# Weights of the weighing read from PSUM, and the last eight tiles weighed ahead of the scores, in a five-pass graph network kernel

## The chip, the cores and the metric

The kernel runs on one core of a Trainium2 chip. The metric is the device time of one execution in microseconds. Before the change the median of three runs is 8032.57 us.

## What is computed

The reference is a stack of four graph layers over 6250 nodes with 256 features each and 106250 edges, sorted by the node they end in. Each layer gathers a 256-wide row for every edge's source, weighs it, sums the rows per destination, and adds a normalised result to the node's features. The layers differ in how the weight of an edge is found. The first and the last use given or degree-based weights. The second is an attention with 8 heads, the third has a 4-head graph attention followed by a 1-head one. Of these two kinds the core is:

```
sim = (q[:, dst] * k[:, src]).sum(-1) * scale        # 8 heads
e   = leaky_relu(es[src] + ed[dst], 0.2)             # 4 heads, then 1 head
m   = segment_max(e, dst);  w = exp(e - m[dst])
out = segment_sum(w * h[src], dst) / segment_sum(w, dst)
```

The change touches the product `w * h[src]` of the 8-head and of the 4-head part.

## The kernel before

The edges are cut into tiles of 128. There are five passes over all tiles, L = 0 to 4: plain sum, 8-head, 4-head, 1-head, plain sum, each followed by a stage over the nodes. The 8-head pass takes the tiles in 55 batches of 16; the 4-head pass takes 27 batches of 32 and a last one of 16.

**The ring.** GpSimd issues one indirect DMA for each tile (line 770), which gathers the 128 source rows into a slot of a ring in SBUF (`ring`, here `rg`). In a slot lie the 256 values and, behind them, columns for the weights of the heads (from `po_` on). Before each group of four gathers GpSimd waits until TensorE has summed the tiles that stood in these slots (`p["agg"]`).

**A batch in the 4-head pass.** The passes are pipelined in software: one step computes the scores of batch b and the sums of batch c = b - 1. The weights go through a chain over four engines:

- VectorE adds up the scores, `scores_of` (lines 1701, 1704, 1706), and signals `s`.
- TensorE turns them into `m0[0:R, 0:128]`, the PSUM bank 6, `turn_scores` (1223, 1224), and signals `st`.
- VectorE scans along the tiles, `ch1` (1785, 1788); TensorE picks rows (1242 to 1244) and signals `row`; VectorE's `ch2` works on them (1805 to 1817); TensorE turns them again (1250, 1251); VectorE's `ch3` (1823 to 1831) leaves the differences from the maxima.
- ScalarE takes the exponential (932, 933, 935), TensorE turns the result back into `m0[:, 128:128 + R]` (`turn_back`, 1256), the other part of the same bank, and ScalarE copies it from there to the ring's weight columns (943) and signals `w`.

In the 8-head pass bank 3 has the part of `m0`, TensorE also spreads the queries over the edges (1188), and VectorE's `pair` multiplies them with the keys (1687) and adds the products up (1678).

**The sums.** VectorE's `begin_sums` (1858, 1859) waits for `w` and for all earlier sums. Then `weigh` (1838) multiplies a tile's values in the ring by its weights, in place, before TensorE multiplies the tile with a one-hot matrix of its destinations (1107). VectorE adds each result to an accumulator in SBUF (1619 in the 4-head pass, 1616 in the 8-head pass). TensorE's sum of tile k waits for the weighing of its group of four (`wv`), for the one-hot, which ScalarE makes (878, 881), and for VectorE's add a few tiles back.

Which engine weighs which tile is written out by hand. In the 4-head pass VectorE weighs all: `prepare_four(g)` is one instruction of 128x1024 for four tiles, `add_and_prepare(g, n)` puts two instructions of 128x512 for group n between the four adds of group g. In the 8-head pass VectorE weighs the first four tiles (`weigh_four(0)`), GpSimd the next four (783) and ScalarE the last eight (909). The 1-head pass has no weighing: there VectorE writes weighted one-hots (`hot_some`).

The order on VectorE in a full step of the 4-head and of the 1-head pass is: `begin_sums`, `prepare_four(0)`, `prepare_four(1)`, sixteen adds with groups 2 to 5 between them, `scores_of`, `prepare_four(6)`, `load_offsets`, `ch1`, adds 16 to 19, `prepare_four(7)`, `ch2`, adds 20 to 23, `ch3`, adds 24 to 31.

TensorE's order is: the sums of tiles 0 to 15, `turn_scores`, sums 16 to 19, the rows for `ch2` (1242 to 1244), sums 20 to 23, the columns for `ch3` (1250, 1251), sums 24 to 27, `turn_back`, sums 28 to 31.

Of the kernel before, what the change touches and what calls it, by code (L numbers as in the profile page):

```python
# [160 lines left out]
def gnn_kernel(nc, a, out):  # L161
    ctx = ExitStack()
    with ctx:
# [1237 lines left out]
        def _(dve):  # L1401
# [158 lines left out]
            for L in range(5):  # L1560
# [87 lines left out]
                else:  # L1648
# [184 lines left out]
                    def weigh(c, rset, k, n):  # L1833

                        four = rg[:, rset * G + k:rset * G + k + n, :]
                        vv = four[:, :, po_ - 256:po_].rearrange("p s (h d) -> p s h d", h=H)
                        wv = four[:, :, po_:po_ + H].unsqueeze(3).to_broadcast([128, n, H, 256 // H])
                        return tt(vv, vv, wv, ALU.mult)  # L1838

                    def hot_some(c, cp, k, n):  # L1840
# [24 lines left out]
                    def batch(i, o, scores, sums):  # L1865
# [38 lines left out]
                        if L == 1:  # L1904
                            pair(0)
                            dots(0)
                            if sums:
                                begin_sums(c, window_at(cp, 0), cp)
                            weigh_four(0)
                            if scores:  # L1910
                                load_offsets(b, par, 0)
                            pair(1)
                            add(0, 1)
                            dots(1)
                            add(1, 3)
                            pair(2)
                            add(3, 4)
                            dots(2)
                            add(4, 5)
                            pair(3)  # L1920
                            add(5, 6)
                            dots(3)
                            add(6, 7)
                            if scores:
                                scan_forward(b, par, ub)
                            add(7, 8)
                            if scores:
                                scan_backward(b, par)
                            add(8, 9)
                            if feed:  # L1930
                                compare_turned(b + 1, (o + 1) % 2)
                            if scores:
                                rows_forward(b, par)
                            add(9, 10)
                            if scores:
                                rows_backward(b, par)
                            add(10, 11)
                            if scores:
                                rows_most(b)
                            add(11, 12)  # L1940
                            if scores:
                                rows_before(b)
                            add(12, 13)
                            if scores:
                                limit_before(b, par)
                            add(13, 14)
                            if scores:
                                limit_behind(b, par)
                            add(14, 15)
                            if scores:  # L1950
                                carry(b)
                            add(15, 16)
                            if scores:
                                differences(b)
                        elif sums and short(L, c):
                            begin_sums(c, window_at(0, 0), cp)
                            prepare_four(0)
                            prepare_four(1)
                            add_and_prepare(0, 2)
                            add_and_prepare(1, 3)  # L1960
                            add(8, 16)
                        else:
                            if sums:
                                begin_sums(c, window_at(0, 0), cp)
                            prepare_four(0)
                            if sums:
                                load_offsets(c, 1, 16)
                            prepare_four(1)
                            add_and_prepare(0, 2)
                            add_and_prepare(1, 3)  # L1970
                            add_and_prepare(2, 4)
                            add_and_prepare(3, 5)
                            if scores:
                                scores_of(b, rset, use, par)
                            prepare_four(6)
                            if scores:
                                load_offsets(b, 0, 0)
                                ch1(b, par, ub)
                            add(16, 20)
                            prepare_four(7)  # L1980
                            if scores:
                                ch2(b, par)
                            add(20, 24)
                            if scores:
                                ch3(b, par)
                            add(24, 32)
# [171 lines left out]
```

## Time and profile before

| | |
|---|---|
| median of the runs | 8032.57 us (8017.61 to 8053.89, three runs) |
| the profiled execution | 8040.43 us |
| its span | 8038.4 us, mean granted TensorE clock 0.76 |
| busy over the span | TensorE 57%, VectorE 54%, GpSimd 58%, ScalarE 31% |
| 8-head pass | about 1637 to 3345 us |
| 4-head pass | about 3552 to 4950 us |
| 1-head pass | about 5130 to 6560 us |

The span is the time from the first to the last record of the profile. What lies around it in the profiled execution is 8040.43 - 8038.4 = 2.0 us. The profiled execution is 7.9 us above the median and lies within the spread of the runs. No engine is busy for more than six tenths of the span, so the time is made of waits of the engines on each other, and the busy shares alone don't say what an instruction on one of them is worth.

### The profile page before, as it was taken

What the parts mean: (1) busy time and instruction counts of PE and PEld (TensorE: products, weight loads), DVE (VectorE), ACT (ScalarE), POOL (GpSimd) and SP (SyncE); (2) the same over time, 40 slices, a digit from 0 to 9 for tenths busy, and PEclk for the clock granted to TensorE, in tenths of its full rate; (3) what the DMA queues carried; (4) which work ended last, traced back from release to release, by engine and by line L of the source; (5) the groups of instructions that cost most, each with busy time, mean ns of one, the idle gap of its engine ahead of it and who ended that gap; (6) DMA issues with size and microseconds to landing.
All of it is one profiled execution on the core that took longest, in us unless ns stands there. A gap on an engine that the chain in (4) does not pass through costs nothing.

```text
span 8038.4 us, 108779 instructions
## 1 busy us (share of the span) xinstructions
PE 4559.5 (57%) x23715; PEld 3453.3 (43%) x23716; DVE 4305.4 (54%) x11140; ACT 2505.5 (31%) x7576; POOL 4682.6 (58%) x5273
## 2 busy tenths in 40 slices
PE   3444446778877787845555556344444463444445
PEld 2444444455555555633333334233333343444444
DVE  4444445567766777735555557344444462444446
ACT  0000000267766777534444445211111130000003
POOL 4666664655555555566666664555555546666661
PEclk6777777889888999967777768667667676777776
DMA  3333332566666666543333333333333343333332
GB/s 87 89 89 89 88 88 70 182 183 197 197 189 183 190 200 189 131 135 112 105 108 109 105 108 63 114 103 100 94 100 102 100 107 107 89 89 88 89 89 85
DMA packets 498682, 953.01 MB, mean 119 GB/s; under 512 B 104802, under 2 KB 298501, under 8 KB 491191
## 3 DMA queue, kind: packets, MB, share of 16 engines
q0 software_dynamic: 235232, 683.41, 31.0%
q1 hardware_dynamic: 263157, 266.87, 10.6%
q14 instruction: 253, 2.07, 0.1%
q8 instruction: 40, 0.66, 0.0%
HBM read 885.36 MB, written 65.90 MB: 118 GB/s over the span
## 4 chain that ended last, share of the span: by engine, by line
PE 37%; DVE 22%; another core or an unknown queue 20%; issue 13%; DVEq 5%; ACT 1%; SPq 1%; DMA 1%; POOL 0%; ACTq 0%; POOLq 0%
PE bank L1107 16%; DVE acc L1635 7%; PE bank L1104 5%; PE bank L1133 4%; DVE ohc L1625 4%; DVE acc L1619 3%; PE bank L1390 2%; PE bank L1186 1%; PE bank L1187 1%; PE bank L1188 1%; DVEq L1604 1%; DVEq L1633 1%; DVE ring L1838 1%; DVE acc L1616 1%
## 5 line engine op out<-in xcount | busy, mean ns | idle before, releaser
L770 POOL DMA_INDIRECT ring<-g_t,stage x1760 | 1736.2, 986 | 1133.0 <-issue 475.8
L1107 PE MATMUL bank<-ring,ohc 128*128 128x264 f32 (+2 forms) x5280 | 1825.2, 477 | 841.7 <-DVE ohc L1843 295.1
L1104 PE MATMUL bank<-ohc,ring 128*128 128x128 f32 x6656 | 1171.6, 352 | 1324.4 <-DVE acc L1635 1233.5
L1104 PEld LDWEIGHTS bank<-ohc,ring 128*128 128x128 f32 x6656 | 1100.4, 260 | 1396.1 <-DVE acc L1635 1305.3
L1107 PEld LDWEIGHTS bank<-ring,ohc 128*128 128x128 f32 x5280 | 1113.4, 235 | 1136.0 <-issue 742.1
L1619 DVE TENSOR_TENSOR acc<-acc,bank 128x261 f32 (+1 forms) x1760 | 747.2, 425 | 1113.5 <-remote 561.4
L770 POOL DMA_INDIRECT ring<-kv_t,stage x880 | 874.8, 994 | 705.3 <-PE bank L1107 409.6
L1625 DVE TENSOR_SCALAR ohc<-iota,rel_c,relx 128x128 f32<-128x128 f32 x1664 | 474.1, 353 | 1183.7 <-remote 878.4
L770 POOL DMA_INDIRECT ring<-in_x,stage x832 | 793.8, 954 | 434.9 <-issue 213.3
L770 POOL DMA_INDIRECT ring<-xs_t,stage x832 | 795.3, 956 | 419.1 <-issue 216.3
L1635 DVE TENSOR_TENSOR acc<-acc,bank 128x256 f32 x1664 | 698.8, 420 | 194.1 <-DVE acc L1635 135.0
L909 ACT ACTIVATE ring<-ring 128x32 f32<-128x32 f32 x3520 | 751.2, 306 | 0.8 <-issue 0.8
L878 ACT ACTIVATE ohc<-iota,rel_c 128x128 f32<-128x128 f32 x1760 | 560.5, 389 | 346.9 <-remote 172.9
L932 ACT ACTIVATE cl<-cl 128x1 f32<-128x1 f32 (+3 forms) x111 | 22.5, 203 | 1960.1 <-issue 916.8
L1133 PE MATMUL bank<-ident 128*128 128x256 bf16 x3410 | 540.7, 292 | 118.4 <-DVE acc L1616 109.1
L1616 DVE SCALAR_TENSOR_TENSOR acc<-acc,aux,bank 128x264 f32 x880 | 423.1, 481 | 314.5 <-PE bank L1107 185.4
L1133 PEld LDWEIGHTS bank<-ident 128*128 128x128 bf16 x3410 | 331.2, 104 | 295.2 <-DVE acc L1616 158.8
L957 ACT ACTIVATE acc<-aux,cols 128x512 f32<-128x512 f32 (+1 forms) x26 | 16.7, 690 | 1294.7 <-DVE aux L2027 1294.7
L961 ACT ACTIVATE acc<-bank 128x512 f32<-128x512 f32 (+1 forms) x13 | 7.4, 573 | 1253.4 <-PE bank L1326 1253.4
L1223 PE MATMUL bank<-ident,sc 128*128 128x128 f32 (+3 forms) x112 | 37.9, 441 | 581.7 <-DVE sc L1706 497.5
L1838 DVE TENSOR_TENSOR ring<-ring 128x512 f32<-128x512 f32 (+1 forms) x385 | 352.8, 917 | 7.2
L1687 DVE TENSOR_TENSOR aux<-bank,ring 128x1024 f32<-128x1024 f32 x220 | 268.5, 1220 | 143.9 <-remote 65.8
(331 smaller groups left out, 6329.5 us busy)
## 6 DMA issues: line engine op xcount, KB each, us to landing
aux<-relb_t SPq DMA_DIRECT2D x56, 1024.0 KB
aux<-q_t SPq DMA_DIRECT2D x880, 64.0 KB
relx<-relb_t SPq DMA_DIRECT2D x55, 512.0 KB
ring<-g_t,stage POOLq DMA_INDIRECT x1760
x<-ring SPq DMA_DIRECT2D x21, 896.0 KB, 4.2
ring<-x SPq DMA_DIRECT2D x21, 896.0 KB, 9.4
mk<-mk SPq DMA_DIRECT2D x445, 32.1 KB
ring<-kv_t,stage POOLq DMA_INDIRECT x880
```

Source lines behind the costliest of these rows:

```text
L770: g_.indirect_dma_start(out=rings[L][:, slot, 0:W], out_offset=None, in_=table[L][:, :], in_offset=bass.IndirectOffsetOnAxis(ap=stage[:, s ...
L878: act.activation(ohc[:, at_k + j, :], iota[:, :], ACT.Abs, scale=-1.0, bias=rel_c[:, ds(c * G + 4 * g + j, 1)])
L909: ins = act.activation(part, part, ACT.Copy, scale=rg[:, cset * G + k, po_ + h:po_ + h + 1])
L1104: ins = mm(banks[k % AB][:, 128 * h:128 * h + 128], rg[:, slot, 128 * h:128 * h + 128], ohc[:, hot, :], start=True, stop=True)
L1107: return mm(banks[k % AB][:, 0:width], ohc[:, hot, :], rg[:, slot, vo:vo + width], start=True, stop=True)
L1133: mm(bank[:, 0:256], filler[:, 0:128], filler[:, :], start=True, stop=True)
L1616: v.scalar_tensor_tensor(win, win, same[:, ds(b * G + k, 1)], agp[k % AGP[L]][:, 0:width], ALU.mult, ALU.add).then_inc(p["added"], 1)
L1619: tt(win, win, agp[k % AGP[L]][:, 0:width], ALU.add).then_inc(p["added"], 1)
L1625: ins = v.tensor_scalar(ohc[:, k % OHS, :], iota[:, :], rel_c[:, k:k + 1], ew_c[:, k:k + 1], ALU.is_equal, ALU.mult)
L1635: tt(win, win, banks[k % 8][:, 0:256].rearrange("p (h n) -> p n h", h=2), ALU.add)\
L1687: tt(prod, qe4[r % 2].rearrange("p (t w) -> p t w", t=4), rg[:, rset * G + 4 * r:rset * G + 4 * r + 4, 0:256], ALU.mult).then_inc(p["prod" ...
L1838: return tt(vv, vv, wv, ALU.mult)
```

## The change

`weigh` takes the weights no longer from the ring's columns but from the PSUM bank, where `turn_back` left them, through a view that turns (head, tile) into (tile, head). ScalarE's copy of the weights to the ring stays (TensorE sums these columns too). In the 4-head pass, `prepare_four(6)` and `prepare_four(7)` both stand ahead of `scores_of`. The 1-head pass keeps its order.

```
@@ -1834,7 +1834,8 @@
                         four = rg[:, rset * G + k:rset * G + k + n, :]
                         vv = four[:, :, po_ - 256:po_].rearrange("p s (h d) -> p s h d", h=H)
-                        wv = four[:, :, po_:po_ + H].unsqueeze(3).to_broadcast([128, n, H, 256 // H])
+                        wts = m0[:, 128:128 + H * tiles_of(L, c)].rearrange("p (h t) -> p t h", h=H)[:, k:k + n, :]
+                        wv = wts.unsqueeze(3).to_broadcast([128, n, H, 256 // H])
                         return tt(vv, vv, wv, ALU.mult)
@@ -1970,14 +1971,19 @@
                             add_and_prepare(3, 5)
+                            if L == 2:
+                                prepare_four(6)
+                                prepare_four(7)
                             if scores:
                                 scores_of(b, rset, use, par)
-                            prepare_four(6)
+                            if L == 3:
+                                prepare_four(6)
                             if scores:
                                 load_offsets(b, 0, 0)
                                 ch1(b, par, ub)
                             add(16, 20)
-                            prepare_four(7)
+                            if L == 3:
+                                prepare_four(7)
                             if scores:
                                 ch2(b, par)
                             add(20, 24)
```

## Rows read from the trace of the kernel before

**Rows 1.** Windows: stretch, length, busy us (xcount) by engine, PEclk; 4-head and 1-head pass.

```profile
3552.00:4950.00 1398.00, 747.29 (x3056) 522.49 (x3057) 761.07 (x1696) 657.81 (x1344) 851.35 (x868) 0.71 0.38 102
5130.00:6560.00 1430.00, 701.51 (x3050) 481.68 (x3051) 687.90 (x2209) 234.16 (x274) 788.60 (x866) 0.70 0.36 95
```

**Rows 2.** Line 1858, first and last start; timeline of VectorE around the last batches.

```profile
L1858 DVE TENSOR_TENSOR acc<-acc,corr x28: 424/426/436, 3570.5 to 4946.6; 128x256 f32 x28
...
4913.52 0.43 DVE L1858 TENSOR_TENSOR acc<-acc,corr 128x256 f32 x1
...
4946.63 0.42 DVE L1858 TENSOR_TENSOR acc<-acc,corr 128x256 f32 x1
```

**Rows 3.** Groups by line and shape, VectorE, 4-head pass: busy us, mean ns, idle before.

```profile
L1838 DVE TENSOR_TENSOR ring<-ring 128x512 f32<-128x512 f32 x216 | 148.0, 685 | 0.0
L1838 DVE TENSOR_TENSOR ring<-ring 128x1024 f32<-128x1024 f32 x110 | 134.6, 1225 | 3.1
L1701 DVE TENSOR_REDUCE sc<-bank 128x128 f32<-128x384 f32 x26 | 14.4, 554 | 1.1 <-issue 0.2
...
L1785 DVE TENSOR_TENSOR_SCAN fw<-mk,bank 128x128 f32<-128x128 f32 x27 | 11.4, 421 | 34.4 <-remote 15.9 <-PE bank L1224 11.7 <-issue 6.8
```

**Rows 4.** Line 1805 in the 4-head pass: what ended VectorE's idle time before it (us, times).

```profile
L1805 DVE TENSOR_TENSOR rows<-bank,cneg_r x28: 200/268/275, 3563.8 to 4936.4; 1x124 f32<-1x124 f32 x27, 1x60 f32<-1x60 f32 x1
...
  PE bank L1244: 3.1, 3
```

**Rows 5.** Timeline of one batch: start us, us, engine line operation [idle before].

```profile
4268.42 0.43 DVE L1619 TENSOR_TENSOR acc<-acc,bank 128x261 f32 x1 [8.89 <-remote]
...
4271.71 0.55 DVE L1701 TENSOR_REDUCE sc<-bank 128x128 f32<-128x384 f32 x1
...
4272.81 0.29 DVE L1706 SCALAR_TENSOR_TENSOR sc<-sc 128x128 f32<-128x128 f32 x1
...
4273.02 1.22 DVE L1838 TENSOR_TENSOR ring<-ring 128x1024 f32<-128x1024 f32 x1
...
4274.02 0.63 PE L1224 MATMUL bank<-mk,ident 128*128 128x128 f32 x2
...
4274.76 0.42 DVE L1785 TENSOR_TENSOR_SCAN fw<-mk,bank 128x128 f32<-128x128 f32 x1 [0.53 <-PE bank L1224]
...
4278.71 0.38 PE L1244 MATMUL bank<-fprow,ones 1*1 1x132 f32 x2
4278.72 1.22 DVE L1838 TENSOR_TENSOR ring<-ring 128x1024 f32<-128x1024 f32 x1
4278.97 1.81 POOL L770 DMA_INDIRECT ring<-g_t,stage  x1 [3.59 <-PE bank L1107]
...
4279.85 0.27 DVE L1805 TENSOR_TENSOR rows<-bank,cneg_r 1x124 f32<-1x124 f32 x1
```

**Rows 6.** Timeline of the first full batch: TensorE's last row matmul and VectorE's ch2.

```profile
3602.08 0.38 PE L1244 MATMUL bank<-fprow,ones 1*1 1x132 f32 x2
...
3604.48 0.27 DVE L1805 TENSOR_TENSOR rows<-bank,cneg_r 1x124 f32<-1x124 f32 x1
```

**Rows 7.** Groups by line, GpSimd: gathers of the 4-head, then of the 8-head pass.

```profile
L770 POOL DMA_INDIRECT ring<-g_t,stage x816 | 836.7, 1025 | 495.4 <-issue 220.8 <-PE bank L1107 166.7 <-remote 108.0
...
L770 POOL DMA_INDIRECT ring<-kv_t,stage x848 | 844.2, 996 | 695.3 <-PE bank L1107 409.6 <-issue 206.8 <-remote 68.9
```

**Rows 8.** Windows of line 770 alone: gathers of the 1-head pass.

```profile
5130.00:6560.00 1430.00, 777.71 (x816) 0.70 0.36 95
```

**Rows 9.** Groups by line and shape, whole span: VectorE's products with a PSUM operand.

```profile
L1687 DVE TENSOR_TENSOR aux<-bank,ring 128x1024 f32<-128x1024 f32 x220 | 268.5, 1220 | 143.9 <-remote 65.8 <-PE bank L1188 65.1 <-issue 11.3
...
L2125 DVE TENSOR_TENSOR ring<-bank,wmore 128x512 f32<-128x512 f32 x49 | 33.9, 691 | 43.8 <-PE bank L1396 43.8
```

**Rows 10.** Timeline of the 8-head pass: the product behind the weighing of 2318.66 us.

```profile
2318.66 1.23 DVE L1838 TENSOR_TENSOR ring<-ring 128x1024 f32<-128x1024 f32 x1
2324.33 1.22 DVE L1687 TENSOR_TENSOR aux<-bank,ring 128x1024 f32<-128x1024 f32 x1 [4.45 <-remote]
```

More of the change, by code:

```diff
@@ L1836, in weigh @@
                         vv = four[:, :, po_ - 256:po_].rearrange("p s (h d) -> p s h d", h=H)
-                        wv = four[:, :, po_:po_ + H].unsqueeze(3).to_broadcast([128, n, H, 256 // H])
+                        wts = m0[:, 128:128 + H * tiles_of(L, c)].rearrange("p (h t) -> p t h", h=H)[:, k:k + n, :]
+                        wv = wts.unsqueeze(3).to_broadcast([128, n, H, 256 // H])
                         return tt(vv, vv, wv, ALU.mult)
@@ L1972, in batch @@
                             add_and_prepare(3, 5)
+                            if L == 2:
+                                prepare_four(6)
+                                prepare_four(7)
                             if scores:
                                 scores_of(b, rset, use, par)
-                            prepare_four(6)
+                            if L == 3:
+                                prepare_four(6)
                             if scores:
@@ L1979, in batch @@
                             add(16, 20)
-                            prepare_four(7)
+                            if L == 3:
+                                prepare_four(7)
                             if scores:
```

## The prediction

> **What bounds the kernel now.** I read the windows by stage first. In the 4-head pass no engine is busy for more than 851 of 1398 us, at a granted TensorE clock of 0.71 [rows 1]. So time goes into waits, and the next question is how the steps repeat. Line 1858, which opens a batch's sums, starts first at 3570.5 and last at 4946.6 us. The last step, 4913.52 to 4946.63, takes 33.1 us and has no gathers left to issue; the 26 before it take (4913.52 - 3570.5) / 26 = 51.7 us each [rows 2]. The 1-head pass has no weighing and is still as long (1430 against 1398 us) [rows 1].
>
> Then the timeline of one batch, to see who hands over to whom [rows 5]. VectorE's score instructions start at 4271.71, with no idle time before them; TensorE's turn starts when line 1706 has ended and lies in PSUM at 4274.02 + 0.63 = 4274.65; VectorE's scan starts at 4274.76. After four adds VectorE weighs group 7 (4278.72) and goes to `ch2` at 4279.85, while TensorE's row was ready at 4278.71 + 0.38 = 4279.09. It is one serial chain VectorE, TensorE, VectorE, ScalarE, and at the end of it stands `w`, without which the next batch's sums don't begin. An instruction put on VectorE inside this chain costs its length unless VectorE would have waited there. In front of line 1701 it waited 0.2 us in the whole pass; in front of line 1785, 34.4 us over 27 times [rows 3]; in front of line 1805 TensorE ended a wait in 3 of 28 cases [rows 4].
>
> Last the gathers. A gather takes 777.71 / 816 = 0.953 us in the 1-head pass [rows 8], 1.025 in the 4-head and 0.996 in the 8-head pass [rows 7]. The one at 4278.97 starts 0.25 us behind a weighing and takes 1.81 us [rows 5]. So a weighing stretches the gather beside it. But GpSimd also sat idle for 495.4 us ahead of its gathers in the 4-head pass and 695.3 in the 8-head pass [rows 7].
>
> **The change, part by part.**
>
> (1) *Where the weights are read.* No row shows a weighing with its weights in PSUM. The nearest rows are products of a PSUM and an SBUF operand: 128x1024 takes 1220 ns, 128x512 takes 691 [rows 9]; the weighing now takes 1225 and 685 [rows 3]. With 165 of the long and 220 of the short in the whole kernel, that is 165 x -5 + 220 x +6 ns = +0.5 us; the two ends are -0.8 and +1.3 us. The new view steps through the bank. Line 1701 does that already: by the slope between the two products, (1220 - 691) / 512 = 1.03 ns an element, 384 contiguous elements would take 691 - 128 x 1.03 = 559 ns, and it takes 554 [rows 3, 9]. So the step costs nothing there, and I take 0. No wait is added: the weighing still stands behind `w`.
>
> The Trainium skill, "VectorE: DVE Perf Modes", section on the TRN2 errata, speaks against this part: it gives a fixed term of 58 cycles from SBUF and 120 from PSUM at 0.96 GHz. That would be an estimated 65 ns on each of the 385 weighings, 25 us in all; the trace disagrees, since 1220 and 1225 ns are the same price.
>
> (2) *The two weighings in front of the scores.* Next to each other they occupy VectorE from 4278.72 to 4279.85, 1.13 us for one [rows 5]. Both stand now where VectorE had no gap, so the scores of 27 steps start 2 x 1.13 = 2.26 us later, 61.0 us in all.
>
> What comes back? The weighing of group 6 ran while TensorE turned the scores, from 4273.02; VectorE still waited 0.53 us behind it for the turn [rows 5]. Its going gives 0. The weighing of group 7 gives back what TensorE's row is early, and at most its length. In the batch shown that is 4279.85 - 4279.09 - 0.10 for the hand-over = 0.66 us [rows 5]; in the first full batch the row is ready at 3602.46 and line 1805 starts at 3604.48, so all 1.13 [rows 6]. Over the 27 steps, worked out in this way, the mean is 0.82 us (ends 0 and 1.13). Sum: 27 x (2.26 - 0.82) = +38.9 us, with ends 27 x 1.13 = +31 and 27 x 2.26 = +61. Queued behind the two weighings on VectorE are only `scores_of` and `ch1`; TensorE waits for them in `turn_scores` with its sums 16 to 31 behind it, and ScalarE's exponential further on, so all of them move together. No DMA moves, and no queue is passed.
>
> (3) *Gathers that are no longer stretched.* If a weighing with only one SBUF input leaves GpSimd alone, the gathers fall to 0.953 us: (1.025 - 0.953) x 816 = 59 us of GpSimd in the 4-head pass and (0.996 - 0.953) x 848 = 36 us in the 8-head pass [rows 7, 8]. In both passes GpSimd has far more idle time than that, ended to a good part by TensorE's sums (166.7 and 409.6 us): it waits for slots to come free, and a shorter gather only makes it wait sooner. I take 0, with -59 and -95 as the other ends.
>
> The Trainium skill, "SBUF — State Buffer", section "Who interferes with whom", says that a VectorE instruction with two SBUF inputs contends with a GpSimd instruction that reads SBUF, and one with a single SBUF input doesn't. By that the stretch would vanish; the trace agrees with the first half (1.81 against 0.95 us) and has no row on a weighing of the second kind.
>
> (4) *8-head pass.* The order stays. One weighing in each of 55 batches changes its source: 55 x -5 ns. Behind it come products that wait anyway (4.45 us at 2324.33) [rows 10].
>
> The sum against the profiled execution is 8040.4 + 38.9 = 8079.3 us (span 8077.3 and 2.0 around it). The profiled execution is 7.9 us above the median of the runs, so on the median it is 8032.6 + 38.9 = 8071.5, forecast 8072 us. The runs spread from 8017.6 to 8053.9, so I call 0.5% (40 us) the least change that can be told from none.
>
> **The rivals.**
>
> *A, the forecast:* the chain sets the time, the order costs 31 to 52 us net. Its own range is 8064 to 8085, and it lies across the border of 0.5% at 8072.7.
>
> *B, faster:* the gathers pace the pass, and their relief shows. For it: a step with gathers takes 51.7 us, one without 33.1 [rows 2]; the 1-head pass with other VectorE work is as long [rows 1]; before the add at 4268.42 VectorE waited 8.89 us for something the profile doesn't name [rows 5]. Against it: the idle time before the gathers. Price: -59 us with the order hidden in such stalls, 7974; with the order's +39 on top, 8013; with the 8-head pass's 36 too, 7938. It decides once more than 39 us of the 59 come through.
>
> *C, no change:* the order is absorbed. If the last adds of a step wait for something with its own pace, as the 8.89 us suggest, a chain that is 1.4 us later ends at the same time: 8033. It decides where that wait is longer than 1.4 us in most steps. Against it: begin of the sums needs `w`, which has come through the whole chain, and ScalarE's and TensorE's waits are on that chain.
>
> *D, slower:* nothing comes back at the old place of group 7, because a four-add stretch that starts at once finds TensorE's row late for another reason (sums 16 to 19 of line 1107 stand ahead of it on TensorE). Then 27 x 2.26 = 61 us, 8094. Against it: the row stood ready 2.02 us early in the first full batch [rows 6], and only 3 of 28 waits were on it [rows 4].
>
> **How the numbers follow.** A 0.40, C 0.25, B 0.22, D 0.13. The predicted time is A's, 8072. The range of 8 in 10: below it lies the better half of B, 0.11, above it half of D, 0.06, which puts it at 7995 to 8096. Slower by over 0.5%: 0.22 of A, which lies across the border, and D's 0.13, together 0.35. Within 0.5%: A's other 0.18 and C's 0.25, together 0.43. Faster by over 0.5%: B's 0.22; its part above 7992 is about made up by C with the 8-head pass's gain.
>
> **What the profile after would show.** Right on (1): line 1838 at 1215 to 1230 and 680 to 695 ns with a bank among its inputs. Right on (2): in front of line 1701 still no idle time; two weighings of 1.13 us ahead of it; idle time before line 1785 unchanged at about 1.3 us a step; waits of line 1805 on line 1244 in most steps, of some 0.3 us; a step of about 53.1 us in place of 51.7. Right on (3): mean gather near 0.95 us in both passes, GpSimd's idle time up by about what its busy time falls. B shows as a step under 51 us with the score instructions just as late behind the start of the sums. C shows as longer VectorE stretches up to line 1701 and shorter waits in the adds of line 1619 in their place. D shows as a 2.3 us longer step and long waits before line 1805.
>
> The prediction is wrong above all if the unexplained stalls of the adds have a pace of their own, since then neither VectorE's order nor its length counts.

## The result

The change made the kernel slower. In the comparison on record the median is 8129.8 us (four runs, 8109.9 to 8159.5) against 8025.1 us before (four runs, 8010.6 to 8053.9); the ratio is 1.0114 with a 95% interval of 1.0075 to 1.0153. That is 92 us more by the ratio, and it lies above the predicted range (7995 to 8096). The same kernel was timed again in three later sessions: 1.0020 (0.9995 to 1.0044), 1.0016 (0.9997 to 1.0035) and 1.0136 (1.0103 to 1.0168). So there are sessions in which the change costs some 15 us and others in which it costs 90 to 110. How the loss comes about in the traces is told below; why the sessions differ stays open. One run of e14 (9262.8 us beside 8121 to 8162) stands apart from all others and is left out of its ratio.

The head of the page of the changed kernel:

```profile
span 8140.3 us, 108779 instructions
## 1 busy us (share of the span) xinstructions
PE 4553.4 (56%) x23715; PEld 3450.0 (42%) x23716; DVE 4303.8 (53%) x11140; ACT 2507.0 (31%) x7576; POOL 4586.4 (56%) x5273
```

The profiled execution took 8142.4 us. VectorE's busy time is what it was (4303.8 against 4305.4), GpSimd's is 96 us less, and the span is 102 us more. GpSimd works less, and the engines wait longer.

The passes, each from the start of its first gather to that of the next pass (worked out from the traces of both kernels, us):

| | plain | 8-head | 4-head | 1-head |
|---|---|---|---|---|
| before | 1477.0 | 1904.2 | 1568.0 | 1619.1 |
| changed | 1474.2 | 1934.4 | 1652.9 | 1613.4 |

85 us of the loss are in the 4-head pass and 30 in the 8-head pass. In the 4-head pass VectorE's busy time changes by 2 us (908.3 to 906.4) and its idle time rises from 737.8 to 822.4 us. That is the whole loss of the pass: 58 us of it stand before the adds, 20 before the scan of line 1785 and 10 before line 1805. The steps, cut at four points, in us (means of 26 steps, worked out from both traces):

| | before | changed |
|---|---|---|
| start of the sums (1858, now 1859) to the scores (1701) | 23.88 | 27.69 |
| scores to the scan (1785) | 3.60 | 3.18 |
| scan to line 1805 | 5.98 | 4.58 |
| line 1805 to the next start of the sums | 18.21 | 19.39 |

The step grew by 3.2 us. The last stretch has no weighing in it before or after, and still it is 1.2 us longer.

The groups of VectorE by line and shape in the 4-head pass now read:

```profile
L1619 DVE TENSOR_TENSOR acc<-acc,bank 128x261 f32 x844 | 360.3, 427 | 578.5 <-remote 323.9 <-PE bank L1107 156.6 <-issue 52.8
L1839 DVE TENSOR_TENSOR ring<-ring,bank 128x512 f32<-128x512 f32 x214 | 145.6, 680 | 0.0
L1839 DVE TENSOR_TENSOR ring<-ring,bank 128x1024 f32<-128x1024 f32 x106 | 126.8, 1217 | 3.2
L1701 DVE TENSOR_REDUCE sc<-bank 128x128 f32<-128x384 f32 x26 | 14.3, 551 | 0.0
...
L1785 DVE TENSOR_TENSOR_SCAN fw<-mk,bank 128x128 f32<-128x128 f32 x27 | 11.4, 421 | 53.4 <-PE bank L1224 35.8 <-remote 12.6 <-issue 5.0
```

The weighing (line 1839 now) reads a bank and costs 1217 and 680 ns where it cost 1225 and 685 [rows 3]. The idle time in front of the adds of line 1619 is the largest figure; the same row of the kernel before, with the same columns:

```profile
L1619 DVE TENSOR_TENSOR acc<-acc,bank 128x261 f32 x865 | 369.3, 427 | 524.5 <-remote 242.2 <-PE bank L1107 173.1 <-issue 59.9
```

GpSimd's gathers, 4-head pass and 8-head pass (they answer to [rows 7]):

```profile
L770 POOL DMA_INDIRECT ring<-g_t,stage x816 | 775.9, 951 | 640.2 <-PE bank L1107 289.3 <-issue 203.7 <-remote 147.1
...
L770 POOL DMA_INDIRECT ring<-kv_t,stage x848 | 820.9, 968 | 717.4 <-PE bank L1107 457.7 <-issue 206.7 <-remote 45.3
```

A gather of the 4-head pass takes 951 ns in place of 1025. The stretch beside the weighings is gone: the gathers that overlap a weighing take 954 ns on average, where they took 1138, and the others 950, where they took 954. GpSimd's idle time rose by 145 us, more than twice the 61 us by which its busy time fell.

Line 1805, what ended VectorE's waits in front of it (answers to [rows 4]):

```profile
L1805 DVE TENSOR_TENSOR rows<-bank,cneg_r x27: 269/275/276, 3590.0 to 5012.5; 1x124 f32<-1x124 f32 x27
...
  PE bank L1244: 16.9, 25
```

In 25 of 27 steps VectorE now waits for TensorE's row, 0.68 us on average; the weighing of group 7 no longer covers this wait.

**Where the loss is made.** The end of one step of the changed kernel, from the timeline:

```profile
4139.73 0.95 POOL L770 DMA_INDIRECT ring<-g_t,stage  x1 [0.30 <-issue]
...
4140.98 0.95 POOL L770 DMA_INDIRECT ring<-g_t,stage  x1 [0.30 <-issue]
4142.23 0.95 POOL L770 DMA_INDIRECT ring<-g_t,stage  x1 [0.30 <-PE bank L1107]
...
4142.71 0.35 ACT L945 ACTIVATE corr<-bank,first_in 128x4 f32<-128x4 f32 x1
4143.28 7.66 SPq L584 DMA_DIRECT2D mk<-mk  x4
4143.48 0.95 POOL L770 DMA_INDIRECT ring<-g_t,stage  x1 [0.30 <-issue]
...
4146.96 0.43 DVE L1619 TENSOR_TENSOR acc<-acc,bank 128x261 f32 x1 [3.83 <-remote]
...
4151.90 1.57 DVE L1619 TENSOR_TENSOR acc<-acc,bank 128x261 f32 x3 [4.51 <-remote]
4152.85 0.94 POOL L770 DMA_INDIRECT ring<-g_t,stage  x1 [3.42 <-remote]
```

The reader is to see three things together. GpSimd issues twelve gathers from 4134.70 to 4148.49, each 1.25 us behind the last, without a pause. SyncE's four loads of the next masks (line 584), issued when `w` comes, take 7.66 us to issue. And in this time VectorE waits 3.83 and then 4.51 us in front of single adds. Such a stretch is called a spell from here on. In a spell the plainest instructions of the queues are slow too: SyncE's line 584 in the 4-head pass, with the least, the median and the longest ns of each operation:

```profile
L584 SPq DMA_DIRECT2D mk<-mk x104: 8/699/1526, 3596.9 to 4966.9; - x104
L584 SPq MOVE mk<-mk x100: 17/697/1396, 3596.8 to 4915.2; - x100
```

A move takes 697 ns at the median. In the kernel before there are both kinds of steps, and the median falls on the other side:

```profile
L584 SPq MOVE mk<-mk x100: 6/38/738, 3570.5 to 4808.0; - x100
```

One step of the kernel before without a spell at the mask loads:

```profile
4603.68 0.95 POOL L770 DMA_INDIRECT ring<-g_t,stage  x1 [1.94 <-issue]
4603.94 1.84 SPq L584 DMA_DIRECT2D mk<-mk  x4
4604.93 0.94 POOL L770 DMA_INDIRECT ring<-g_t,stage  x1 [0.30 <-issue]
```

Here GpSimd had just paused for 1.94 us, and the same four loads are issued in 1.84 us. The mask loads are one gauge of a spell, measured from the register operation in front of them to the end of the fourth: 17 of 25 steps of the kernel before need over 5 us, and 24 of 25 steps of the changed kernel, in each of its four profiles. A second spell lies in many steps in front of the add of tile 12 (counted from 0). The adds' waits of over 3 us sum to 216 us in the 4-head pass before and to 339 us after. Their shorter waits fell, though, from 311 to 246 us, so all idle time before the adds rose by 58 us only.

Whether the mask loads are slow goes with the place in a burst of gathers where they fall. Counting the gathers since GpSimd's last pause of over 0.7 us, they begin at the first or second in six steps of the kernel before, all fast, and at the seventh or eighth in 15, all slow. In the changed kernel no step has them at the first four: 23 of the 24 slow ones begin at the fifth to eighth. The long bursts themselves did not become more: 320 gathers of the kernel before stand seventh or later in their burst, and 261 of the changed kernel (without the first 64).

### The profile page after: what moved, and what is told of

It is laid out like the page before. It is cut to its first block, busy times and chain, and to the rows that moved or that the text cites. A ratio compares the mean times of both kernels' runs of the same rounds, so it can differ in the third digit from the quotient of the medians.

```text
span 8140.3 us, 108779 instructions
## 1 busy us (share of the span) xinstructions
PE 4553.4 (56%) x23715; PEld 3450.0 (42%) x23716; DVE 4303.8 (53%) x11140; ACT 2507.0 (31%) x7576; POOL 4586.4 (56%) x5273
## 4 chain that ended last, share of the span: by engine, by line
PE 34%; another core or an unknown queue 22%; DVE 22%; issue 13%; DVEq 5%; ACT 2%; ACTq 1%; SPq 1%; DMA 1%; POOL 0%; POOLq 0%
PE bank L1107 16%; DVE acc L1635 8%; DVE ohc L1625 5%; PE bank L1133 4%; PE bank L1104 3%; DVE acc L1619 3%; PE bank L1390 2%; DVE ring L1839 1%; DVEq L1604 1%; DVEq L1633 1%; PE bank L1186 1%; PE bank L1187 1%; PE bank L1188 1%; DVE acc L1616 1%
## 5 line engine op out<-in xcount | busy, mean ns | idle before, releaser
L770 POOL DMA_INDIRECT ring<-g_t,stage x1760 | 1672.2, 950 | 1276.9 <-PE bank L1107 521.1
L1107 PE MATMUL bank<-ring,ohc 128*128 128x264 f32 (+2 forms) x5280 | 1763.0, 465 | 943.9 <-DVE ohc L1844 304.9
L1104 PE MATMUL bank<-ohc,ring 128*128 128x128 f32 x6656 | 1209.8, 357 | 1280.4 <-DVE acc L1635 1173.4
L1104 PEld LDWEIGHTS bank<-ohc,ring 128*128 128x128 f32 x6656 | 1122.9, 264 | 1367.7 <-DVE acc L1635 1262.6
L1107 PEld LDWEIGHTS bank<-ring,ohc 128*128 128x128 f32 x5280 | 1083.9, 229 | 1215.1 <-issue 847.2
L770 POOL DMA_INDIRECT ring<-kv_t,stage x880 | 852.0, 968 | 727.3 <-PE bank L1107 457.7
L1839 DVE TENSOR_TENSOR ring<-ring,bank 128x512 f32<-128x512 f32 (+1 forms) x385 | 348.4, 911 | 7.4
```

The source lines that it names most:

```text
L770: g_.indirect_dma_start(out=rings[L][:, slot, 0:W], out_offset=None, in_=table[L][:, :], in_offset=bass.IndirectOffsetOnAxis(ap=stage[:, s ...
L1104: ins = mm(banks[k % AB][:, 128 * h:128 * h + 128], rg[:, slot, 128 * h:128 * h + 128], ohc[:, hot, :], start=True, stop=True)
L1107: return mm(banks[k % AB][:, 0:width], ohc[:, hot, :], rg[:, slot, vo:vo + width], start=True, stop=True)
```

## The experiments

The theory formed from these traces, B: after some seven gathers without a pause, the engines' queues slow down for 5 to 10 us, and the order of the weighings matters less by its own length than by the bursts of gathers that it leaves. Its rivals: O, the order alone makes the loss; G, the unstretched gathers make it; S, the spells belong to SyncE's loads or the program's order, whatever the gathers do. Ratios are to the kernel before in the same session, with the 95% interval. "Long waits" are the adds' waits of over 3 us in the 4-head pass; "spells" the steps of 25 whose mask loads take over 5 us, as measured above; "slow" the moves and register operations of the SyncE, ScalarE and TensorE queues that take 0.6 to 2 us, out of some 3440 between the 65th gather of the pass and its last 16; "4-head" is the pass measured as in the table above. The three columns of the pass come from one profile each. The kernel before has a profile only from the session of the comparison; in the session of e1 to e4, e3 stands for it, since its 4-head pass is that of the kernel before. On record e1 to e4 ran on one chip, e5 to e8 on a second, e9 to e12 on a third and e13 to e15 on a fourth.

| run | ratio | 4-head, us | long waits, us | spells | slow |
|---|---|---|---|---|---|
| kernel before | 1 | 1568.0 | 216 | 17 | 98 |
| changed, on record | 1.0114 (1.0075 to 1.0153) | 1652.9 | 339 | 24 | 192 |
| e1 order only | 1.0061 (1.0041 to 1.0081) | 1644.2 | 352 | 24 | 208 |
| e2 PSUM, old places | 0.9931 (0.9906 to 0.9955) | 1544.4 | 173 | 8 | 114 |
| e3 PSUM in 8-head only | 0.9997 (0.9978 to 1.0016) | 1566.8 | 220 | 18 | 108 |
| e4 change again | 1.0020 (0.9995 to 1.0044) | 1611.9 | 293 | 24 | 216 |
| e5 landed, before | 1.0339 (1.0285 to 1.0393) | 1803.9 | 0 | 0 | 25 |
| e6 landed, change | 1.0272 (1.0218 to 1.0327) | 1763.6 | 0 | 0 | 29 |
| e7 spaced, before | 0.9882 (0.9832 to 0.9932) | 1469.4 | 188 | 17 | 113 |
| e8 spaced, change | 1.0037 (1.0005 to 1.0070) | 1587.6 | 251 | 24 | 169 |
| e9 group 6 ahead | 0.9955 (0.9937 to 0.9973) | 1560.7 | 177 | 14 | 146 |
| e10 change, third | 1.0016 (0.9997 to 1.0035) | 1590.1 | 258 | 24 | 212 |
| e11 spaced, PSUM | 0.9923 (0.9901 to 0.9944) | 1560.9 | 234 | 21 | 128 |
| e12 pause each eight | 0.9968 (0.9949 to 0.9988) | 1561.9 | 121 | 19 | 182 |
| e13 group 7 ahead | 1.0015 (0.9992 to 1.0039) | 1571.9 | 247 | 20 | 163 |
| e14 change, fourth | 1.0136 (1.0103 to 1.0168) | 1629.1 | 312 | 24 | 185 |
| e15 PSUM, old places, again | 1.0000 (0.9976 to 1.0024) | 1578.4 | 266 | 18 | 110 |

### The parts of the change: e1 to e4

**e1.** The new order, with the weights read from the ring:

```
-wts = m0[:, 128:128 + H * tiles_of(L, c)].rearrange(...)[:, k:k + n, :]
-wv = wts.unsqueeze(3).to_broadcast(...)
+wv = four[:, :, po_:po_ + H].unsqueeze(3).to_broadcast(...)
```

> Groups 6 and 7 are weighed ahead of the scores as in the change, but all weights are still read from the ring in SBUF. If the order alone makes the loss (theory O), this run is as slow as the change: 80 to 105 us above the kernel before. If the order costs what was forecast, 27 steps by 1.44 us, it is 39 us above. If the loss comes with the gathers that are no longer stretched (theory G), at most those 39 us are seen here, and the mean gather of the 4-head pass stays near 1.02 us.

Measured: 8072.8 against 8012.9 us, ratio 1.0061: 49 us by the ratio. The mean gather of the 4-head pass is 994 ns. That is near the forecast of 39 us for the order and under O's 80. It doesn't decide O, though: in the session of e1 to e4 the whole change costs 16 us (e4), so e1 is slower than the change. The spells are at 24 of 25.

**e2.** The PSUM weights without the new order. Group 6 must keep the ring there, since TensorE writes into its bank meanwhile (the turn of the scores) and nothing orders the two. For that reason the plain form, all weights from PSUM in the old order, is not among the runs.

```
+if L == 2 and k == 24:
+    wts = four[:, :, po_:po_ + H]
+else:
+    wts = m0[:, 128:128 + H * tiles_of(L, c)].rearrange(...)[:, k:k + n, :]
```

> All weighings read PSUM but that of group 6 in the 4-head pass, which keeps reading the ring; all stand at their old places. Theory O: within 10 us of the kernel before. Theory G: 40 to 65 us above it, with the mean gather at 0.95 to 0.96 us in the 4-head pass. If shorter gathers help: 20 us or more below.

Measured: 7970.8 us (seven runs), ratio 0.9931, 55 us faster. G falls (unstretched gathers by themselves don't slow the kernel), and in the session of e1 to e4 the forecast's 0 for the gathers falls too. It is the first version that beats both kernels. Gathers take 961 ns, and only 8 of 25 steps have the spell at the mask loads. The same kernel in another session (e15) has neither the gain nor this count.

**e3.** PSUM weights for `L == 1` alone, old order.

> Only the one weighing of each batch in the 8-head pass reads PSUM; the 4-head pass is as before. The profile of the changed kernel has an 8-head pass 30 us longer than that of before. Theory G: 20 to 30 us above the kernel before. Theory O: no change, within 10 us, and the 30 us were scatter between executions.

Measured: 8017.1 us, ratio 0.9997. The 8-head weighing's source is worth nothing that can be told from 0, though its gathers fell from 994 to 971 ns.

**e4.** The changed kernel, unaltered.

> The change itself, beside the others on the same chip: 92 us above the kernel before by the first comparison (ratio 1.0114), with a second profile of it, to see which of the stage lengths repeat: 4-head pass plus 85 us, 8-head pass plus 30 us, the other three within 6 us.

Measured: 8037.2 us, twelve runs, ratio 1.0020. The second profile has a 4-head pass of 1611.9 us and an 8-head pass of 1876.8 us. So of the stage lengths only the sign of the first repeats; the 30 us of the 8-head pass don't show here. Against e3's profile the 4-head pass is 45 us longer and the 1-head pass, whose code the change leaves alone, 30 us shorter (1588.8 and 1618.7); e10 shows the same, 1590.1 and 1591.6. Why the 1-head pass gains is open. The kernel before, e1, e2 and e4, all timed in one session, make a square. The order costs 49 us with weights from the ring (e1) and (1.0020 - 0.9931) x 8013 = 71 us with weights from PSUM (e2 to e4). PSUM weights gain 55 us in the old order and (1.0061 - 1.0020) x 8013 = 33 us in the new one. The intervals are some 16 to 20 us wide to each side for each ratio, so whether the two parts add can't be told. (e2 keeps group 6 on the ring, e4 doesn't.)

### Gathers and spells: e5 to e8

**e5, e6.** In the 4-head pass GpSimd starts each group of four gathers only when the one before has landed; on the kernel before (e5) and on the changed one (e6).

```
 if g == 0:
     pool.wait_ge(p["staged"], ...)
+if L == 2:
+    f = s * 4 + g
+    if f:
+        pool.wait_ge(s_ring[f - 1], i * 64 + (64 + ring_base(L, f - 1)))
+    else:
+        pool.wait_ge(s_ring[15], i * 64 + ring_base(L, 15))
```

> The kernel before, with one wait added in the 4-head pass: GpSimd starts a group of four gathers only when the group before has landed. No burst of gathers is longer than four. Theory B (bursts: after six or more gathers without a pause all sequencers slow to about 0.7 us an instruction for 5 to 8 us): these spells vanish from the 4-head pass, the adds' idle time of over 3 us falls from 216 us to under 60, and the kernel is 80 to 250 us faster. Rival S (the spells belong to SyncE's DMA issues or to the program's order, whatever the gathers do): the spells stay, and the kernel is 0 to 150 us slower by the gathers' later landing.

> The change with the same wait. Theory B: with the spells gone the change costs only the order's length on VectorE's path, so this run is 25 to 50 us above the one with the wait on the kernel before (forecast 39), and below the kernel before. Rival S: the change stands to that run as it did to the kernel before, 20 to 90 us above, with the spells in its trace.

Measured: 8295.7 us (1.0339) and 8243.3 us (1.0272). GpSimd's timeline of e5:

```profile
4105.20 0.95 POOL L776 DMA_INDIRECT ring<-g_t,stage  x1 [2.58 <-DMA ring<-g_t,stage]
4106.45 0.94 POOL L776 DMA_INDIRECT ring<-g_t,stage  x1 [0.31 <-issue]
4107.70 0.95 POOL L776 DMA_INDIRECT ring<-g_t,stage  x1 [0.30 <-issue]
4108.95 0.95 POOL L776 DMA_INDIRECT ring<-g_t,stage  x1 [0.30 <-issue]
4112.44 0.95 POOL L776 DMA_INDIRECT ring<-g_t,stage  x1 [2.53 <-issue]
```

Four gathers take from 4105.20 to 4112.44, 7.2 us, so a step's eight groups take 58, and the steps are 61.4 us long: GpSimd is now the bound. Both time forecasts of B are wrong (80 to 250 us faster for e5, measured 272 slower; e6 25 to 50 us above e5, measured 52 below). What B said of the spells is right. The adds of e5 by group:

```profile
L1625 DVE TENSOR_TENSOR acc<-acc,bank 128x261 f32 x880 | 375.1, 426 | 171.3 <-PE bank L1113 103.8 <-DVE acc L1625 11.9 <-issue 6.9
```

The idle time before all 880 adds fell from 527.5 us to 171.3, no wait is over 3 us, and the mask loads take over 5 us in no step. SyncE's moves of line 584 stand at 29 ns at the median, where the kernel before has 38; more telling, 11 of the pass's 104 moves take 0.6 us or more in place of 43, and the slow operations fall from 98 to 25:

```profile
L584 SPq MOVE mk<-mk x100: 4/29/705, 3559.9 to 5030.0; - x100
```

Since SyncE's loads and the order of the program are those of the kernel before, S falls: the gathers' timing makes the spells. But e5 changes two things at once, the longest burst and the gathers' mean pace (a gather every 1.9 us in place of 1.6), so by itself it doesn't show that the length of a burst is the cause. And with the wait in both kernels the change is the faster one, by 52 us. The gathers by group, e5 and then e6:

```profile
L776 POOL DMA_INDIRECT ring<-g_t,stage x852 | 849.6, 997 | 771.2 <-issue 605.3 <-DMA ring<-g_t,stage 153.1 <-PE bank L1113 12.8
```

```profile
L776 POOL DMA_INDIRECT ring<-g_t,stage x852 | 808.1, 948 | 775.2 <-issue 601.5 <-DMA ring<-g_t,stage 155.3 <-PE bank L1113 18.3
```

849.6 - 808.1 = 41.5 us less GpSimd time, and the 4-head pass is 40.3 us shorter (1803.9 and 1763.6): this is rival B of the prediction, at nearly full price, in the one place where gathers do set the pace. The order's cost doesn't show there.

**e7, e8.** A small GpSimd copy behind each gather of the 4-head pass, into columns of the slot that nothing reads; on the kernel before and on the changed one.

```
+if L in (2,):
+    g_.tensor_copy(rings[L][:, slot, 261:264], rel_c[:, 0:3])
```

> The kernel before, with a small GpSimd copy behind each gather of the 4-head pass (three columns of the slot that nothing reads), so that the gathers of a burst start about 1.5 to 1.8 us apart in place of 1.25. Theory B in the form that the rate of issue matters: the spells grow rare, 50 to 200 us faster. If only the number of gathers without a real pause matters: the spells stay, and it is 0 to 60 us slower.

> The change with the same copies. Rate of issue matters: within 25 to 50 us above the spaced kernel before. Otherwise: above it by as much as the change is above the kernel before, 20 to 90 us, and the spells sit in its trace at the seventh to twelfth gather of a burst, as in the change.

Measured: 7929.9 us (0.9882) and 8065.9 us (1.0037). The spacing shortens the 4-head pass of the kernel before by 99 us, and the largest gain of the study (95 us) is this one line. But it doesn't remove the spells (17 steps again, many of them just over 5 us; 113 slow operations; long waits 188 us): some steps have 15 us or more of waits, and nine of 26, of 36 to 47 us, have none over 3 us. e7's profile is of its slowest run (7986 us), with an 8-head pass of 1968.8 us. On the changed kernel the copies gain less: the change was not run without them in the session of e5 to e8, but in the comparison on record and in e14 it stood at 1.0114 and 1.0136, with a 4-head pass of 1652.9 and 1629.1 us against 1587.6 here. The order and the PSUM weights together then cost more than ever, 1587.6 - 1469.4 = 118 us in the pass and (1.0037 - 0.9882) x 8023 = 124 us by the ratios, outside both forecasts of e8. The rate of issue alone isn't the cause.

### Which group costs, and the sessions: e9 to e15

**e9** has group 6 ahead of the scores and group 7 at its old place; **e13** has group 7 ahead, and group 6 at its old place and from the ring.

```
 if L == 2:
     prepare_four(6)
-    prepare_four(7)
 ...
-if L == 3:
-    prepare_four(7)
+prepare_four(7)
```

> The change with group 7 back at its old place; only group 6 is weighed ahead of the scores, and all weights come from PSUM. By the forecast's prices: 2.26 - 0.82 us less 1.13 - 0 us: the move of group 7 costs 0.31 us a step, that of group 6 1.13 us, so this run should be 8 us under the change and 31 us above the run with PSUM and the old places (0.993 of the kernel before), near 8000. Theory B (the order matters by the length of the gather bursts that it leaves): more than half of the 70 us between that run and the change hangs on one of the two groups, together with the idle time of the adds.

> As e2 (PSUM weights, group 6 from the ring at its old place), with group 7 alone weighed ahead of the scores. By the forecast's prices it costs 27 x (1.13 - 0.82) = 8 us over e2: 7975 to 7985. Theory G7 (group 7 behind ch1 broke up the last bursts of gathers, since it held back VectorE's adds and with them TensorE's sums and the free slots): 40 to 60 us over e2, close to the change, with 20 or more spells at adds 28 and 29. Theory T (it takes the length of both, 2.26 us): 15 to 30 us over e2, as group 6 alone.

Measured: e9 7989.2 us, 0.9955, which is (0.9955 - 0.9931) x 8020 = 19 us over e2, which ran in another session (forecast for group 6: 1.13 x 27 = 31). e13 8063.9 us, 1.0015, which is 12 us over e15 (forecast for group 7: 8). Theory G7 asked for 40 to 60 us and falls. By the intervals of the ratios both differences are uncertain by some 25 us either way, so they agree with the forecast's prices and also with 0. The two groups together, against none, cost 71 us in one session (e4 and e2) and (1.0136 - 1.0000) x 8045 = 109 us in another (e14 and e15). Against 19 + 12 that looks like more than a sum, but each group alone was run in one kind of session only. The traces point the same way: with one group the mask loads are slow in 14 and 20 steps, with both in 24 of 25; the slow operations are 98 to 114 with none ahead (kernel before, e2, e3, e15), 146 and 163 with one, and 185 to 216 with both.

**e10** and **e14** are the changed kernel once more, **e15** is e2 once more.

> The change itself once more, since its two comparisons gave 1.0114 and 1.0020. If they differ by the chip or the session, a third ratio between 1.000 and 1.013; if the first four runs were a tail of one distribution, again 1.000 to 1.005. The step of the 4-head pass has a long spell at adds 28 to 29 in nearly every step; how many steps have the one at adds 9 to 12 decides between 8030 and 8130.

> The change itself in another session. If the session decides: a ratio outside 1.000 to 1.005 is possible again. If the first four runs were a tail: 1.000 to 1.005, all runs below 8080 but for one or two.

> The version with PSUM weights at the old places again, to settle its gain: 0.990 to 0.996 of the kernel before. If the gain was of one session only: 0.997 to 1.003.

Measured: 1.0016, 1.0136 and 1.0000. The forecast of e15, 0.990 to 0.996, missed; its other case, a gain of one session only, came out. The first comparison was no tail: the session decides. The sessions part in two kinds that the traces show as well. In those of e1 to e4 and e9 to e12 the 8-head pass takes 1857 to 1886 us in all eight profiles; in those of the comparison on record, e5 to e8 and e13 to e15 it takes 1904 to 1969 us in all nine. In the first kind the change costs 0.2% and e2 gains 0.7%; in the second the change costs 1.1 to 1.4% and e2's kernel, run there once (e15), gains nothing. So in the second kind the loss is the new order's (with group 6's weights, which e15 keeps on the ring): e14 less e15. Every session of the runs was on another chip, so a difference of chips and one of sessions can't be told apart. The spells don't make the difference: the change has as many slow operations in the first kind (216 and 212) as in the second (192 and 185).

**e11, e12.** e2 with the copies in the 4-head and the 1-head pass; e2 with the wait for landing in front of each second group of four.

> PSUM weights at the old places (as e2), with the small GpSimd copy behind each gather of the 4-head pass and of the 1-head pass as well. If the gains of both add: 0.993 and 0.988 give about 0.981, 7870 us, and the 1-head pass shortens too. If spacing helped only by breaking one pattern of bursts: 0.985 to 1.00, with the 1-head pass within 15 us of 1615.

> As e2, and GpSimd waits for the landing of all gathers before each second group of four in the 4-head pass, so no burst is longer than eight. Gathers need 32 x 1.25 + 4 x 2.5 = 50 us a step by themselves, so the pass can't be shorter than 27 x 50 = 1350 us and a tail. Theory B: few spells, a step of 50 to 53 us, within 30 us of the kernel before. If spells don't care for the length of a burst: the two add, 100 us or more above it.

Measured: 7944.0 us (0.9923), and 7988.1 us (0.9968). In e11 the gains don't add: the copies bring the 1-head pass to 1561.7 us, from 1591.6 to 1613.4 in the other profiles of its session, but the 4-head pass is 16 us longer than in e2. In e12 the long waits are down to 121 us and the adds' idle time to 337 us, and the pass is no shorter (1561.9), since gathers and pauses fill the step, as expected. But B's few spells did not come: 19 of 25 steps still have one, and 182 queue operations are slow, against 98 in the kernel before, 63 of them at the first six gathers of a burst. So a pause at every eighth gather moves the spells and doesn't end them, and "after some seven gathers" is not the rule.

## Why the prediction was wrong

**The weighing's price** (part 1) was right: taken as unchanged, measured 8 and 5 ns less. The fixed term of the Trainium skill's page "VectorE: DVE Perf Modes", section on the TRN2 errata, would have given an estimated 25 us more; no row of the changed kernel shows it (1217 and 680 ns).

**The two weighings ahead of the scores** (part 2) were right in what they do to VectorE's queue. The scores follow the start of the sums 3.8 us later than before; 2.26 of that are the weighings, and the other 1.5 are waits of the adds, which no term of the sum held. More came back than was let come back: 1.40 us between the scan and line 1805, where the sum had 0.82, and 0.42 before the scan, where it had 0. By this count the weighings alone would have left 2.26 - 1.40 - 0.42 = 0.44 us a step, an estimate of some 12 us in the pass. With the ring the order costs 49 us (e1) against the 38.9 predicted. One reading was off without harm: before line 1701 VectorE's idle time was 1.1 us in the pass, of which 0.2 is the part with a named end. Two signs were off: the idle time before line 1785 rose from 1.3 to 2.0 us a step, and the wait for the row is 0.68 us, not 0.3.

**The gathers that are no longer stretched** (part 3) were taken at 0. The stretch vanished as said (951 ns). In the second kind of session, that of the comparison, 0 is what e15 shows (1.0000). In the first kind PSUM weights are worth -55 us in the old order (e2), near the forecast's end of -59, and -33 in the new one (e1 to e4); where gathers are the bound they are worth their full length (e6). GpSimd's idle time rose by more than twice what its busy time fell, since the pass itself got longer. This term doesn't make the loss. The rule of the Trainium skill's page "SBUF — State Buffer", section "Who interferes with whom", held on the half that no row had shown: with one SBUF input, the weighing doesn't lengthen a gather.

**The failed step** is the assumption of the sum that everything it didn't name stays as it was: "Its own range is 8064 to 8085" rests on it. The adds' long waits were seen (rival C named the 8.89 us) and taken either as fixed or as a cushion that swallows the order's 39 us. The runs showed them to be neither. Of the 3.2 us by which a step grew, the weighings leave 0.4 by the count above; the other 2.7 us are 1.5 us more in the stretch of adds ahead of the scores and 1.2 us in the stretch behind line 1805, in which no weighing stands. That is some 74 of the pass's 85 us. The long waits grew from 216 to 339 us, 113 of the 123 in the last eight adds of the steps. Within a kind of session they move with the order: 173 us (e2) and 220 (e3) against 258 to 352 (e1, e4, e10) in the first kind, 216 and 266 (kernel before, e15) against 312 and 339 in the second. They are gone in e5 and e6, where a group of gathers waits for the landing of the one before.

What links order and waits is shown in part. The gathers' timing makes the spells (e5), and in the changed kernel the mask loads no longer meet a fresh burst, as they did in six steps before. A mechanism for this fits, argued and not shown: with both groups ready early, TensorE's last sums run closer together, their slots come free at once, and GpSimd issues its last twelve gathers without the pause that had let the mask loads through. That long bursts as such are the cause doesn't hold: the change has fewer gathers late in a burst (261 against 320), e7 has 492 and is the fastest kernel, and e12, with bursts of eight at most, has about as many slow operations as the change (182 and 192).

The forecast's middle, +39 us, was less than half of the cost in one kind of session (92 and 109 us) and over twice the cost in the other (13 and 16 us), where e2's gain pays most of the order. That the second kind is so much dearer stays open. That the range ended at 8096 was the second fault: its upper end was the order's full length, 61 us, as if nothing but VectorE's own time could get longer.

**The 8-head pass** (part 4) was taken at 0 and is 30 us longer in the profiles on record. Its weighing isn't the cause: e3, e13 and e15 have it from PSUM, at a ratio of 0.9997 (e3) and with a pass of 1907 us (e13, e15). It is 1931 to 1942 us in all four profiles that have the whole change in the second kind of session and 1904 to 1918 in e5, e13, e15 and the kernel before, but 1969 in e7, which has none of the change. What makes the difference stays open.

## What to carry to other kernels

Before costing an edit on the critical chain, explain the long waits that the profile doesn't name. If they hang on another queue's timing, an edit can move them; here they grew by 123 us, where the range allowed the order its own length, 61 us. Then account for the idle time by line after the change, short waits too: here the long ones grew by 123 us and all before the adds by 58. A queue that is "off the path" by its idle time can still cost time by when it issues; a small filler in it (95 us faster here for one line) is worth trying before any reordering. And time an edit of half a per cent in more than one session and on more than one chip.

## What was not expected of the hardware

- While a spell lasts, moves and register operations of SyncE's, ScalarE's and TensorE's queues take about 0.70 us each, moves 0.03 elsewhere. In the changed kernel's 4-head pass 191 of the 192 slow operations fall at the seventh to twelfth gather of a burst (counted from the last pause of over 0.7 us), and the last at the sixth. Elsewhere the position is not so firm: in e2 31 of 114 fall at the first six, in e12 63 of 182, and in e5, whose bursts end at four, all 25, each of them on SyncE. The DMA engines had no backlog then: over the step from 4099 to 4157 us of the changed kernel a gather's bytes had been moved 1.3 us after GpSimd's instruction ended in most cases, and 3.2 us at most. What it is that slows the queues, no run tells.
- The median of the kernel before differs by 0.4% or less between sessions (8012.9 to 8045.2 us), and what the same edit does to it by over 1% (ratios of 1.0016 to 1.0136). Each of the four sessions of e1 to e15 was on a chip of its own.
